# Attention scores in two row tiles of 64 rows, and x2 written over x

## The reference

```python
x = x + layernorm(attention(layernorm(x), WQ, WK, WV, WO))
#   scores = Q K^T / sqrt(8), masked above the diagonal; softmax over keys; times V; times WO
x = x + layernorm(ffn(layernorm(x), centroids, ...))
#   aff = x @ centroids.T; the expert is argmax(aff); alpha = sigmoid(aff of that expert)
#   h = relu(layernorm(x)*g + b @ w1.T + b1); ye = x + h @ w2.T + b2; out = alpha*ye + (1-alpha)*x
```

## Time and profile before

| | |
|---|---|
| median of the runs | 412.28 us |
| profiled execution | 413.59 us, span 411.8 us |
| TensorE busy | 331.5 us (80%) |
| VectorE busy | 326.3 us (79%) |
| ScalarE busy | 237.3 us (58%) |
| GpSimd busy | 241.3 us (59%) |
| mean granted clock of TensorE | 0.942 |
| queue q1 (loads and stores by SyncE and ScalarE) | 37.43 MB, 45.0% of 16 engines |

### The profile page before, as it was taken

One profiled execution on the slowest core, in us unless ns is written; L12 is line 12 of the kernel. 1 busy time (PEld: TensorE's weight loads), 2 busy tenths in 40 slices (PEclk: granted clock), 3 DMA queues, 4 the chain that ended last, 5 costly groups with the idle time before them and its releaser, 6 DMA issues.

```text
span 411.8 us, 11210 instructions
## 1 busy us (share of the span) xinstructions
PE 331.5 (80%) x3642; PEld 265.7 (65%) x3642; DVE 326.3 (79%) x1215; ACT 237.3 (58%) x574; POOL 241.3 (59%) x337
## 2 busy tenths in 40 slices
PE   2447989999999999999999999987512999999940
PEld 1225667776776676776777766754412999889930
DVE  7846788879789798898898898886481899999980
ACT  2202566586575674674864766556212798889840
POOL 4831364564474574674765756648560188878783
PEclk9998999999999999999999999999555999999985
DMA  7572674554544635626535436112026666766610
GB/s 217 104 121 51 92 164 87 89 114 85 90 98 62 102 76 69 116 63 87 102 75 80 102 73 101 32 35 65 22 71 176 166 176 189 206 182 183 194 31 6
DMA packets 34681, 42.78 MB, mean 104 GB/s; under 512 B 5465, under 2 KB 25053, under 8 KB 33088
## 3 DMA queue, kind: packets, MB, share of 16 engines
q1 hardware_dynamic: 31744, 37.43, 45.0%
q0 software_dynamic: 2304, 4.37, 3.3%
q10 hardware_dynamic: 576, 0.27, 0.2%
HBM read 30.59 MB, written 11.66 MB: 103 GB/s over the span
## 4 chain that ended last, share of the span: by engine, by line
PE 44%; DVE 21%; issue 12%; POOL 8%; DMA 7%; ACT 4%; SPq 2%; POOLq 0%; DVEq 0%; ACTq 0%
PE S L836 5%; DVE nmf L1112 5%; PE O L870 4%; PE MB L796 4%; POOL out_x L539 3%; PE ST L849 3%; PE S L831 3%; PE MB L884 2%; PE ST L858 2%; DVE res L1100 2%; DMA aug<-qk_parts 2%; PE O L874 2%; PE S L1017 2%; POOL rsz L549 2%; PE S L829 2%
## 5 line engine op out<-in xcount | busy, mean ns | idle before, releaser
L1112 DVE TENSOR_REDUCE nmf<-S 128x2 f32<-128x512 f32 (+1 forms) x192 | 129.5, 682 | 38.4 <-PE S L836 31.4
L608 ACT ACTIVATE p<-ST 128x1024 f32<-128x1024 f32 x64 | 65.5, 1023 | 29.5 <-PE ST L849 29.5
L446 POOL TENSOR_SCALAR_AFFINE_SELECT p<-p 128x512 f32<-128x512 f32 x64 | 40.7, 636 | 42.9 <-ACT p L612 42.4
L442 POOL TENSOR_SCALAR_AFFINE_SELECT p<-p 128x512 f32<-128x512 f32 x64 | 40.5, 633 | 28.7 <-ACT p L608 28.6
L836 PE MATMUL S<-aug 126*128 126x128 bf16 x512 | 50.6, 221 | 0.0
L539 POOL DMA_INDIRECT out_x<-vaug,x_all x39 | 42.0, 1077 | 7.9 <-issue 7.7
L836 PEld LDWEIGHTS S<-aug 126*128 126x128 bf16 x512 | 40.3, 99 | 2.1
L870 PE MATMUL O<-p,vaug 128*32 128x256 f32 x512 | 41.1, 390 | 0.6 <-POOL p L442 0.6
L472 POOL DMA_INDIRECT xs_rows<-pay,pos x32 | 32.2, 1005 | 14.2 <-DVE pay L1257 6.5
L436 POOL TENSOR_TENSOR qkp<-res,qkp 128x512 bf16<-128x512 f32 x16 | 18.5, 1157 | 36.7 <-ACT qkp L582 36.7
L849 PE MATMUL ST<-aug 128*128 128x256 bf16 x256 | 38.5, 272 | 1.9 <-ACT p L608 0.7
(11 more groups left out here) (163 smaller groups left out, 861.7 us busy)
## 6 DMA issues: line engine op xcount, KB each, us to landing
w1s<-in_w1x SPq DMA_DIRECT2D x39, 259.0 KB
qk_parts<-qkp SPq DMA_DIRECT2D x16, 384.0 KB
aug<-qk_parts SPq DMA_DIRECT2D x32, 192.0 KB
aug<-qk_parts SPq DMA_DIRECT2D x32, 128.0 KB
x_all<-xs_rows SPq DMA_DIRECT2D x39, 67.0 KB
aug<-qk_parts SPq DMA_DIRECT2D x32, 64.0 KB
w_tab<-in_w2t SPq DMA_DIRECT2D x8, 256.0 KB
out_x<-vaug,x_all POOLq DMA_INDIRECT x39
```

The source lines that it names most:

```text
L442: g.affine_select(out=v, in_=v, compare_op=ALU.is_ge, fill=0.0, base=0, pattern=[[0, 4], [1, P]], channel_multiplier=-1).then_inc(s["sel0" ...
L446: g.affine_select(out=v, in_=v, compare_op=ALU.is_ge, fill=0.0, base=0, pattern=[[0, 4], [1, P]], channel_multiplier=-1).then_inc(s["sel1" ...
L608: a.activation(p0[:, gr % 2], ST0[:, :, :], ACT.Exp, scale=SCALE).then_inc(s["exp0"], 1)
L1112: v.tensor_reduce(dst, S[:, n % 2].rearrange("p (j n) -> p j n", j=k), op=ALU.max, axis=AX_X, negate=True).then_inc(s["red"], 1)
```

## The change

Heads 0 to 7 keep their 48 rows on partitions 0 to 47 and heads 8 to 15 theirs on partitions 64 to 111, with the shift in two rows after each. A product of `scores_by_query` has 48 rows, one of the near and far scores 50. Products of the two halves follow each other in turn and write different banks, except in `scores_far`, whose one bank is written by one half first and later by the other (`st1_a`). `scores_by_query` is called for a block m (0 to 5) that fills both banks of `S`, and the order of TensorE's stream is new. `qaug` needs no zeros; `parts_in` makes twelve loads of half the size, `shift` two. `pay` is gone: x2 and its scalars are written over x in `x_all`, whose rows have 134 fields now; the token's numbers are put there once. In the steps without a batch `t`, GpSimd computes the second power ahead of the scatters. The rows of the weights for Q and K are reordered on the host.

```diff
-    SHIFT = P - 2
+    HALF = P // 2
+    SHIFT = 6 * DH
-        x_all = sb("x_all", [P, NT, D])
-        pay = sb("pay", [P, RING, 2, ROW])
+        x_all = sb("x_all", [P, NT, ROW])
-        aug = sb("aug", [P, 2 * RING * NH * SEQ], BF16)
+        aug = sb("aug", [P, RING * NH * SEQ], BF16)
...
-                row = 0
-                for n in (3, 2, 1):
-                    rows = n * DH
-                    sp.dma_start(qaug[row:row + rows, p], qk_dram[p, 0, 0:n].rearrange("c d h t -> (c d) h t"))\
...
+                for g in (0, 1):
+                    row, heads = HALF * g, slice(NH // 2 * g, NH // 2 * (g + 1))
+                    for n in (3, 2, 1):
+                        rows = n * DH
+                        sp.dma_start(qaug[row:row + rows, p], qk_dram[p, 0, 0:n, :, heads].rearrange("c d h t -> (c d) h t"))\
+                            .then_inc(aug_in[p], 16)
...
                 if ln:
                     power(ln, 0)
+                if ln and not t:
+                    power(ln, 1)
...
-                if ln:
+                if ln and t:
                     power(ln, 1)
-                    number(ln)
...
-            def scores_by_query(b, gr, u):
...
+            def scores_by_query(b, m):
+
+                p, half = b.slot(RING), m // 3
+                if m == 0:
+                    pe.wait_ge(aug_in[p], b.turns(RING, 192, 192))
+                for g in (0, 1):
+                    if b.k > 0 or m > 0:
+                        pe.wait_ge(s["red"], b.times(12, 2 * m + g - 1))
+                    if m % 3 == 0:
+                        mm(S[:, g], identb[:, :], causal[:, :, :], start=True, stop=False)
+                    else:
+                        mm(S[:, g].rearrange("p (j c n) -> p j c n", j=2, c=2)[:, :, 1], identb[:, :], causal[:, 0:2],
+                           start=True, stop=False)
+                for n in range(4):
+                    for g in (0, 1):
+                        q, k = tile_rows(qaug, p, g, SHIFT), tile_rows(kaug, p, g, SHIFT)
+                        if m % 3 == 0:
+                            j = 4 * half + n
+                            ins = mm(S[:, g, n * P:(n + 1) * P], q[:, j, 0:P], k[:, j, 0:P], start=False, stop=(n == 3))
+                        else:
+                            j, kb = 4 * half + 2 * (m % 3 - 1) + n // 2, n % 2
+                            ins = mm(S[:, g, n * P:(n + 1) * P], q[:, j, P:SEQ], k[:, j, kb * P:(kb + 1) * P],
+                                     start=False, stop=(n == 3))
+                        if n == 3:
+                            ins.then_inc(s["s_r"], 1)
...
-                for j in range(4):
-                    h = 4 * gr + j
-                    last = mm(ST0[:, j], kaug[:, p, h, 0:P], qaug[:, p, h], start=True, stop=True)
+                for jj in (0, 1):
+                    for g in (0, 1):
+                        q, k = tile_rows(qaug, p, g, SHIFT + 2), tile_rows(kaug, p, g, SHIFT + 2)
+                        last = mm(ST0[:, 2 * g + jj], k[:, 2 * gr + jj, 0:P], q[:, 2 * gr + jj], start=True, stop=True)
                 last.then_inc(s["st0_r"], 1)
 
-            def scores_far(i, gr):
+            def scores_far(i, gr, g):
+
                 p = i.slot(RING)
-                if i.k > 0 or gr > 0:
+                if g == 0 and (i.k > 0 or gr > 0):
                     pe.wait_ge(s["exp1"], i.times(NG, gr))
+                if g == 1:
+                    pe.wait_ge(s["st1_a"], i.times(NG, gr + 1))
+                for jj in (0, 1):
...
```

More of the change, by code:

```diff
@@ L314, in parts_in @@
                     sp.wait_ge(s["st1_r"], b.times(NG, -NG * (RING - 1)))
-                row = 0
-                for n in (3, 2, 1):
-                    rows = n * DH
-                    sp.dma_start(qaug[row:row + rows, p], qk_dram[p, 0, 0:n].rearrange("c d h t -> (c d) h t"))\
[L319 to L322, removed]
+                for g in (0, 1):
[4 more added lines that the diff above has]
+                            .then_inc(aug_in[p], 16)
+                        sp.dma_start(kaug[row:row + rows, p], qk_dram[p, 1, 3 - n:3, :, heads].rearrange("c d h t -> (c d) h t"))\
+                            .then_inc(aug_in[p], 16)
+                        row += rows
             def shift(b, half):
@@ L337, in _ @@
             parts_out(Nth(1))
-            sp.wait_ge(s["qzero"], 3)
             sp.wait_ge(s["kone"], 3)
@@ L908, in transpose_f @@
                 for t in (0, 1):
-                    last = nc.tensor.transpose(MA[:, t * P:(t + 1) * P], pay[:, i.slot(RING), t, 0:D], ident[:, :])
+                    last = nc.tensor.transpose(MA[:, t * P:(t + 1) * P], x_row(i, t), ident[:, :])
                 last.then_inc(s["fT_r"], 1)
@@ L945, in _ @@
             for gr in range(NG):
-                for u in range(3):
-                    scores_by_query(Nth(0), gr, u)
+                for m in ((0, 1), (2,), (3, 4), (5,))[gr]:
+                    scores_by_query(Nth(0), m)
                 if gr == 1:
@@ L958, in step @@
                         scores_near(t, gr)
+                        scores_far(t, gr, 0)
                     if nxt:
-                        scores_by_query(nxt, gr, 0)
-                    if gr == 0 and l2:
+                        scores_by_query(nxt, (0, 2, 3, 5)[gr])
+                    if gr == 0 and l2 and not nxt:
+                        project_o(l2)
+                    if gr == 1 and not nxt:
+                        affinities_and_ranks(i.plus(-3), ln, last)
+                    if gr == 2 and t and not nxt:
+                        weigh_values(t, 1)
+                    if gr == 3 and old and not nxt:
+                        transpose_on(old)
+                    if t:
+                        scores_far(t, gr, 1)
+                    if gr == 0 and t:
+                        transpose_shift(t, 1)
+                    if gr == 0 and l2 and nxt:
                         project_o(l2)
@@ L964, in step @@
                         centroid_sums()
-                    if gr == 1 and (ln or last):
+                    if gr == 1 and (ln or last) and nxt:
                         affinities_and_ranks(i.plus(-3), ln, last)
+                    if gr == 3 and old and nxt:
+                        transpose_on(old)
+                    if gr == 0 and old:
+                        weigh_values(old, 3)
+                    if gr in (1, 3) and t or gr == 2 and t and nxt:
+                        weigh_values(t, gr - 1)
+                    if gr == 0 and ln:
+                        transpose_f(ln)
+                    if gr == 1 and new:
+                        transpose_x(new)
+                    if gr == 1 and old:
+                        transpose_o(old)
                     if gr == 2 and nxt:
@@ L1196, in add_y @@
                 dve.wait_ge(s["ln_rs"], b.times(2, 1))
-                if b.follows(RING) or p == FIRST_SCAT:
-                    dve.wait_ge(scat[p], b.turns(RING, 32, 16 * (p == FIRST_SCAT)))
                 for t in (0, 1):
-                    last = v.scalar_tensor_tensor(out=pay[:, p, t, 0:D], in0=yb[:, p, t], scalar=rs_y[:, t:t + 1],
-                                                  in1=b.pick(x_all, 1, 2, t).rearrange("p o d -> p (o d)"),
-                                                  op0=ALU.mult, op1=ALU.add)
+                    last = v.scalar_tensor_tensor(out=x_row(b, t), in0=yb[:, p, t], scalar=rs_y[:, t:t + 1],
+                                                  in1=x_row(b, t), op0=ALU.mult, op1=ALU.add)
                 last.then_inc(s["x2_d"], 1)
@@ L1512 @@
     e, f, _ = L0_ffn_w1.shape
-    attn_w = np.stack([np.asarray(w).transpose(2, 1, 0).reshape(d, nh * dh) for w in (L0_attn_WQ, L0_attn_WK)]
+    attn_w = np.stack([np.asarray(w).reshape(4, 2, 2, dh, d).transpose(4, 3, 1, 0, 2).reshape(d, nh * dh)
+                       for w in (L0_attn_WQ, L0_attn_WK)]
                       + [np.asarray(L0_attn_WV).reshape(nh * dh, d).T]
```

154 lines of the change are left out of this document (57 added, 97 removed).

## The result

The changed kernel takes **503.45 us** (median of 5 runs, 490.66 to 521.36) against 412.27 beside it. The ratio is 1.1986, 95% interval 1.1925 to 1.2047; it is formed without the runs that lie over 1.5% above the fastest of their kernel, which leaves two of the changed one, 490.66 and 496.67 (middle 493.7). The profiled execution is the fastest, 490.66 us. The forecast was 446, the range 424 to 468: the direction was right, the time lies far outside.

What follows compares the result with a forecast made beforehand. TensorE was taken to set the 16.09 us step, VectorE 2.3 us behind. Fifteen steps at 2.2 us more (+33) and the rest (+1) made +34 on 413.59, 447.6, shown as a 446 us median; range 424 to 468.

Steps and rivals of the forecast that it cites:

- Overlap of the tiles, full: Score products in two row tiles overlap fully: a block's eight cost 0.23 us instead of 0.45; 2.2 us less TensorE per step.
- 0.10 for a change of tiling: On TensorE each change between whole array, column tiles and row tiles costs 0.10 us; about 14 more a step, 1.4 us.
- The six intervals, 18.4 us a step: TensorE's times from one block's last product to the next block's sum to 18.4 us against 16.09, 2.3 more a step.
- the two stalls behind ScalarE: Half of far on TensorE waits for exp_far: 0.5 us between blocks 2 and 3, 0.8 us at a step's start.
- The rest, +1: Extra loads and the six blocks ahead of the loop: together +1 us (-1 to +4); reordered last four steps 0.
- The start: Later loads for the first batch and lost alternation ahead of the loop: +1 us; first two steps 2.2 us each.
- VectorE-bound, 397: Rival: eased TensorE reaches blocks before VectorE empties their banks; VectorE sets a 15.0 us step, 397 us; chance 0.08.
- The third rival, "The clock falls": TensorE's clock falls as its busy share sinks; one step in five slow, 3 us a step more, 490 us; chance 0.07.

Runs made afterwards that it cites:

- experiment 1: Changed kernel, but while blocks 2 and 5 wait for bank 1, bank 0's mask is written again 5 and 10 times; 456.68 us, ratio 1.1093.
- experiment 2: Changed kernel's order, double blocks and waits, but products on the whole array (126 and 128 rows) and six part loads; 460.63 us, ratio 1.1167.
- experiment 5: Kernel of experiment 1 with exp_far(1) ahead of xnT and exp_far(3) ahead of v_out on ScalarE; 440.64 us, ratio 1.0646.
- experiment 4: Everything of the change but the scores, on the scores and TensorE order of the kernel before; 415.23 us, ratio 1.0087.
- 3: Row tiles in the order of the kernel before: twelve one-bank blocks, each in one tile, near paired, far in two parts; two runs 435.3, two 449.3 us.
- 6: Kernel of experiment 1 with a block's two reductions back to back on VectorE, small operations behind the pair; 452.56 us, ratio 1.0941.
- 7: Changed kernel, no filling, exp_far(1) and exp_far(3) earlier on ScalarE, blocks 2 and 5 later, behind affinities or values; 418.26 us, ratio 1.0121.
- experiment 8: Changed kernel with exp_far(1), exp_far(3) and exp_near(3) earlier on ScalarE, blocks 2 and 5 later, reductions paired, no filling; 413.34 us, ratio 1.0024.

## Why the prediction was wrong

By spans, from the sums of the 14 steps (before 222.9 us, filled 259.25, after 292.0):

| | before to filled (1) | filled to after |
|---|---|---|
| up to the first of the 14 steps | +7.0 | +2.6 |
| 14 steps | +36.4 | +32.8 |
| what follows | -1.0 | -0.6 |
| span | 411.8 to 454.1 | 454.1 to 488.9 |

Step by step of the prediction:

- **Overlap of the tiles, full:** right. Eight products take 0.24 us, near 0.22.
- **0.10 for a change of tiling:** right, 0.09.
- **The six intervals, 18.4 us a step:** right, 18.72, each within 0.2 us. The order makes them and not the tiling (experiment 2: 18.77); the two stalls behind ScalarE are real, and worth 1.26 (experiment 5).
- **The rest, +1:** within its bounds (-1 to +4), +3 by experiment 4, though in good part for a reason that was costed as hidden: the second shift load. The prediction let the shifts fit into a step of 16 us and did not ask when near wants them. In the changed kernel itself near waits for no shift load (its new order brings near later), so these 3 us can't be added to the rest.
- **The start:** mis-sized. The prediction gave it +1 and the first steps 2.2 each; the first of the 14 steps begins 7.0 us later with filled waits and 9.6 without. It is hardly the tiles or the twelve loads: experiment 2 has the new order without either, and its first of the 14 steps begins at 61.12 us, that of the changed kernel at 61.22. From 20 to 60 us TensorE's masks wait 6.9 us for VectorE's reductions, 6.4 in experiment 2, 2.1 before. The rest is at least in part the clock: masks of 256 columns take 0.39 us until 48 us in the after trace.
- **VectorE-bound, 397:** nowhere. It is 64% busy.
- **The third rival, "The clock falls":** this is the step that failed. It was given 0.07, sized as one slow step in five, and left out of the range. The profile shows a third of the time at the lower level, 93 us, which costs 35 us of span against experiment 1 (37 from the 493.7, 47 in the medians). Its 490 was the nearest of all the numbers given. Its price of 3 us a step was about right: 2.3 over the 14 steps of the two traces (32.8 / 14), 2.5 to 3.1 by the times (37 and 47 over 15). Its chance was not. The prediction had its evidence: a busy share that sinks to three quarters, and waits of 0.5 to 1.5 us in a row in each step. It set no cost of the waits against them, and spread the missing time over one step in five without a row to say so.

What made the clock fall can be narrowed, not settled:

| | rows of a product | waits | clock of the steps |
|---|---|---|---|
| after | 48, 50 | as forecast | 0.64 to 0.97, the last two 1.00 |
| 1 | 48, 50 | two of them filled | 1.00, in one 0.91 |
| 2 | 126, 128 | as forecast | 1.00, in four 0.92 to 0.97 |
| 3 | 48, 50, one tile at a time | short | 1.00 (two runs without a trace lower) |
| 5, 6 | 48, 50 | two filled, one kind shortened | 1.00, the first 0.83 and 0.84, one late 0.91 |
| 7 | 48, 50 | short | 1.00, the first 0.75 |

A fall as deep as in the changed kernel came only with both, the tiled products and the standstills; with either alone it came seldom or not at all in the traces kept. The Trainium skill (TensorE: Matmul & The Clock Gate, "A second HAM failure mode: psum-queue depth-cycling") tells of a kernel in which frequent short pauses between groups of products made the clock swing between its levels; the after trace agrees, with waits of at most 1.43 us in the step shown. Whether it is the fewer rows of a product that matter or the shorter time that the pairs take, no run here tells apart.

## What to carry to other kernels

Two banks that are filled together and emptied together are one bank: the alternation was worth more than the halved products, and only with other work put between the blocks again did the tiles show their gain (0.34 us a step), a small part of what their halved product times promise. When a change shortens TensorE's work and adds waits of 0.4 to 1.4 us in the same loop, cost the whole step once more with TensorE at half clock, and give that case a real chance. When a loop's rhythm is measured, the fill of the pipeline has to be costed by itself: experiment 8 wins 0.87 us in each steady step and gives all of it back before the second.

## What was not expected of the hardware

- A standstill can be shorter than the slow stretch that follows it by far: after 1.43 us of waiting the clock stayed at its lower level for some 10 us. Redundant masks in the gap, 7% more instructions in a step (203 for 189), made the kernel 37 us faster (47 in the medians).
- Two tiny DMAs for one (4 KB each) took SyncE 1.28 us to issue instead of 0.62, and in experiment 4 that reached TensorE in the first step.
- Up to its first recorded change the clock's row reads 1.00, though masks of 256 columns took 0.39 to 0.40 us (0.28 at full clock). Early in a trace the length of a known product is the better clock.
